# The last graph turn written out by hand, part of its routing moved into slices between the first expert units, unit rows in 38 buffers, landings looked up for 24 units

## The reference

```python
x = x + gnn(layernorm(x), adj, adj, ...)          # x: 128 graphs x 128 nodes x 128
# origin = where(adj <= 0, adj, 1); gnn: relu(((origin*adj) h + edge) * sigmoid(h g1 + b1)
#   + ((origin.T*adj) h + edge2) * sigmoid(h g2 + b2) + h * sigmoid(h g3))
xf = layernorm(x).reshape(-1, 128)                # 16384 tokens
top_w, top_i = top_k(xf @ Wg + bg, 2)             # the two largest of 8 logits
top_w = softmax(top_w)
for e in range(8):
    h = gelu(xf @ W1[e] + b1[e])                  # 128 -> 512, exact gelu
    out += w_dense[:, e:e+1] * (h @ W2[e] + b2[e])
return x + out
```

## Time and profile before

| | before |
|---|---|
| median of three runs | 720.95 us |
| the profiled execution, its time | 719.69 us |
| its span, first to last instruction | 717.8 us |
| busy: PE, DVE, ACT, POOL | 654.3, 608.5, 541.3, 504.2 us |
| share of the span on the chain that ended last: PE, ACT, POOL, issue, DMA, DVE | 32%, 23%, 13%, 12%, 10%, 8% |
| graph stage, to the first unit's layer 1 on PE | 0 to 214 us |
| first copy of a unit's output (`y_t`) | 225.88 us |
| DMA | 161.06 MB, 224 GB/s over the span |

### The profile page before, as it was taken

The page is one execution under the profiler, slowest core; times in us unless marked ns, Lnnn a source line. Parts: engine busy times, 40 slices in busy tenths (PEclk is TensorE's granted clock), DMA queues, the critical chain, the costliest instruction groups (busy, mean ns, idle before and its releaser), DMA issues.

```text
span 717.8 us, 17809 instructions
## 1 busy us (share of the span) xinstructions
PE 654.3 (91%) x4879; PEld 596.8 (83%) x4879; DVE 608.5 (85%) x2041; ACT 541.3 (75%) x1505; POOL 504.2 (70%) x471
## 2 busy tenths in 40 slices
PE   5979898988859999899997999988999999999991
PEld 4646566666539999899997999988999999999991
DVE  5899999999986888987885888885888888888881
ACT  4689999999977978788674767664777776767670
POOL 2553777676764577778887888877777777777774
PEclk9999999999977999999998999998999999999997
DMA  8999995558346897959999975789764444444211
GB/s 293 336 357 279 354 345 180 178 177 309 107 148 182 288 327 254 310 163 300 325 353 319 370 240 159 219 320 354 241 160 128 122 129 120 125 128 125 72 42 33
DMA packets 85497, 161.06 MB, mean 224 GB/s; under 512 B 32631, under 2 KB 36736, under 8 KB 85392
## 3 DMA queue, kind: packets, MB, share of 16 engines
q1 hardware_dynamic: 66032, 112.96, 50.2%
q0 software_dynamic: 18496, 46.70, 17.8%
q10 hardware_dynamic: 864, 0.21, 0.1%
HBM read 104.95 MB, written 57.23 MB: 226 GB/s over the span
## 4 chain that ended last, share of the span: by engine, by line
PE 32%; ACT 23%; POOL 13%; issue 12%; DMA 10%; DVE 8%; SPq 1%; POOLq 0%; DVEq 0%; ACTq 0%
POOL out_dram L688 8%; ACT hs L750 6%; POOL rows L691 5%; ACT row L759 5%; ACT t_loop L741 4%; PE bank L1623 4%; PE bank L1624 4%; PE bank L1625 4%; PE bank L1637 4%; PE bank L1638 4%; PE bank L1642 4%; ACT t_in L734 3%; DMA rows<-row,to_row 3%; PE bank L1609 2%; PE bank L1653 2%
## 5 line engine op out<-in xcount | busy, mean ns | idle before, releaser
L846 ACT ACTIVATE act_f<-bank,b_t 128x256 f32<-128x256 f32 x560 | 220.1, 476 | 22.8 <-PE bank L1625 14.7
L688 POOL DMA_INDIRECT out_dram<-row,to_row x140 | 165.7, 1184 | 57.7 <-issue 56.1
L646 POOL DMA_INDIRECT rows<-row,slot_low x128 | 136.8, 1069 | 62.6 <-issue 34.4
L1429 DVE TENSOR_TENSOR act_lo<-act_f,act_hi 128x1024 fp32r<-128x1024 f32 x140 | 171.9, 1228 | 5.9 <-ACT act_hi L852 0.2
L1422 DVE CAST act_hi<-act_f 128x1024 fp32r<-128x1024 f32 (+1 forms) x140 | 90.5, 647 | 70.1 <-ACT act_f L846 67.7
L836 ACT ACTIVATE in_hi<-bank 128x256 fp32r<-128x256 f32 x140 | 53.9, 385 | 113.4 <-PE bank L1609 113.1
L1623 PE MATMUL bank<-in_hi,w_t 128*128 128x256 f32 x376 | 115.6, 308 | 7.5 <-DMA w_t<-w_split 7.5
L691 POOL DMA_INDIRECT rows<-row,to_row x76 | 94.6, 1245 | 24.7 <-issue 20.9
L1624 PE MATMUL bank<-in_lo,w_t 128*128 128x256 f32 x376 | 107.4, 286 | 0.0
L1625 PE MATMUL bank<-in_hi,w_t 128*128 128x256 f32 x376 | 107.4, 286 | 0.0
L1637 PE MATMUL bank<-act_hi,w_t 128*128 128x256 f32 x376 | 100.9, 302 | 0.1
(11 more groups left out here) (278 smaller groups left out, 1762.2 us busy)
## 6 DMA issues: line engine op xcount, KB each, us to landing
row<-rows SPq DMA_DIRECT2D x108, 260.0 KB, 3.0
w_t<-w_split SPq DMA_DIRECT2D x52, 512.0 KB, 6.3
w_up<-w_split SPq DMA_DIRECT2D x28, 512.0 KB, 6.1
xs<-in_x_dram SPq DMA_DIRECT2D x16, 512.0 KB, 4.7
x_t<-in_x_turned_dram SPq DMA_DIRECT2D x16, 512.0 KB, 6.3
rows<-ends_rep SPq DMA_DIRECT2D x15, 260.0 KB, 7.7
xs<-rows SPq DMA_DIRECT2D x10, 260.0 KB
b_t<-in_biases_dram SPq DMA_DIRECT2D x140, 2.5 KB
```

What stands on the lines that cost most here:

```text
L646: pool.indirect_dma_start(out=rows, out_offset=bass.IndirectOffsetOnAxis(ap=slot_low[:, r, b:b + 1], axis=0), in_=row[:, r, b, :], in_offs ...
L688: pool.indirect_dma_start(out=out_rows, out_offset=at, in_=got[:, g, j, P:2 * P], in_offset=None, bounds_check=TOKENS - 1, oob_is_err=Fals ...
L846: last = act.activation(act_f[:, s, c, :], ps_h(t, half)[:, i, :], ACT.Gelu, bias=b_t[:, w, c:c + 1])
L1429: dve.tensor_tensor(act_lo[:, s], act_f[:, t.slot(2)], act_hi[:, s].bitcast(F32), ALU.subtract).then_inc(s_hlo, 1)
```

## The change

The last turn of the graph pipeline, which still held routing of chunk 12 and norms of chunk 14, is written out on PE, ACT and DVE without them. That work goes into the slices: the list on DVE is spread over k = 0 to 26 and has chunk 12's maxima (4), places (5), counts (6) and rows (7) in it, the norms of chunks 14 and 15 are done together (3), and chunk 13, 14 and 15 come later than before. NE becomes 34. Buffers for unit rows become 38 (LANES): 22 (FIRST) for the first 34 units in turn, and then all 38 in turn. For units 4 to 7 DVE casts the whole hidden layer, where ACT casts half of it for the other first units. On GpSimd the rows of chunk 12 come behind unit 4, the others are put elsewhere, and the landing of a unit is waited for and counted five units later in place of three. EARLY becomes 24.

```diff
-    EARLY = 3 * GR // 4
+    EARLY = 24
...
-    NE = 2 * GR
+    NE = 4 * FULL - (E - 2)
+    FIRST = 22
+    LANES = FIRST + GR
...
+    def lane(k):
+        return k % FIRST if k < NE else (FIRST + k - NE) % LANES
+    def uses(k):
+        return sum(lane(i) == lane(k) for i in range(k))
+    def halved(k):
+        return k < NE and not 4 <= k < 8
...
                     g = t.slot(GR)
-                    if not NE <= t.index < NE + GR:
-                        wait_slot(sp, s_out, 16 * BLK, t, 0)
+                    if uses(t.index):
+                        sp.wait_ge(s_out[lane(t.index)], 16 * BLK * uses(t.index))
...
-            now = entries(0, 0, NE, MOST, held=full_table)
+            now = entries(0, 0, UT, MOST, held=full_table) + entries(0, UT, NE - UT, MOST, held=full_table)
...
-            for k in range(CHUNKS - 3):
+            for k in range(CHUNKS - 4):
                 scatter_rows(chunk(k))
...
             def landed(t):
-                wait_slot(pool, s_out, 16 * BLK, t, 16 * BLK)
+                pool.wait_ge(s_out[lane(t.index)], 16 * BLK * (uses(t.index) + 1))
                 pool.sem_inc(s_landed, 1)
...
-                if 0 <= t.index - 3 < NU:
-                    landed(t.back(3))
+                if 0 <= t.index - 5 < NU:
+                    landed(t.back(5))
                 wait_turn(pool, s_done, 1, t, 1)
...
-            for k in range(6):
+            for k in range(5):
+                scatter(unit(k))
+            scatter_rows(chunk(CHUNKS - 4))
+            for k in range(5, 8):
                 scatter(unit(k))
             scatter_rows(chunk(CHUNKS - 3))
-            for k in range(6, 10):
+            for k in range(8, 11):
                 scatter(unit(k))
             scatter_rows(chunk(CHUNKS - 2))
-            for k in range(10, 14):
+            for k in range(11, 13):
                 scatter(unit(k))
             scatter_rows(chunk(CHUNKS - 1))
-            for k in range(14, UNITS):
+            for k in range(13, UNITS):
                 scatter(unit(k))
...
+            def last_turn(t):
+                two = t.back(1)
...
+                place_ranks(chunk(CHUNKS - 5))
+                place_rows(chunk(CHUNKS - 5))
+                for k in range(2):
...
+                    dve.tensor_tensor(t_sum[:, half, :], t_sum[:, half, :], t_loop[:, half, :], ALU.add).then_inc(s_tout, 1)
+                    if k == 0:
+                        wait_turn(dve, s_logit, 1, chunk(CHUNKS - 4), 1)
+                        dve.tensor_copy(full_table[:], ps_full_table).then_inc(s_full_tab, 1)
...
                 if k == 0:
                     last_sums(chunk(CHUNKS - 1))
                 elif k == 1:
+                    last_stats(chunk(CHUNKS - 2))
+                elif k == 2:
+                    last_stats(chunk(CHUNKS - 1))
+                elif k == 3:
+                    last_norms()
+                elif k == 4:
+                    last_maxima(chunk(CHUNKS - 4))
+                elif k == 5:
+                    last_two(chunk(CHUNKS - 4))
+                elif k == 6:
                     last_logits(chunk(CHUNKS - 3))
-                    last_stats(chunk(CHUNKS - 1))
...
+                    last_counts(chunk(CHUNKS - 4))
+                elif k == 7:
+                    place_ranks(chunk(CHUNKS - 4))
+                    place_rows(chunk(CHUNKS - 4))
```

More of the change, by code:

```diff
@@ L400, in program @@
         s_done = sem("unit_summed")
-        s_out = [sem(f"unit_rows_scattered{i}") for i in range(GR)]
+        s_out = [sem(f"unit_rows_scattered{i}") for i in range(LANES)]
         s_landed = sem("first_pass_units_landed")
@@ L600, in _ @@
                         rows_in(unit(k + AHEAD), early[k + AHEAD - NU] if 0 <= k + AHEAD - NU < AHEAD else now[i])
-            for i in range(GR):
-                sp.wait_ge(s_out[i], 16 * BLK * ((UNITS + GR - 1 - i) // GR))
+            for k in range(UNITS - LANES, UNITS):
+                sp.wait_ge(s_out[lane(k)], 16 * BLK * (uses(k) + 1))
         @block.gpsimd
@@ L1166, in full_units @@
                 dve.scalar_tensor_tensor(out=full_code[:, 0:1], in0=start_, scalar=16.0, in1=new_, op0=ALU.mult, op1=ALU.add).then_inc(s_full_code, 1)
-            for k in range(CHUNKS + 2):
+            for k in range(CHUNKS + 1):
                 until = turn(chunk(k), until)
@@ L1420, in hidden_hi @@
                 wait_turn(dve, s_act, 2, t, 2)
-                done = FC // 2 if t.index < NE else 0
+                done = FC // 2 if halved(t.index) else 0
                 dve.tensor_copy(act_hi[:, t.slot(LATE + 1), done:], act_f[:, t.slot(2), done:]).then_inc(s_hhi, 1)
@@ L1426, in hidden_lo @@
                 wait_turn(dve, s_hhi, 1, t, 1)
-                if t.index < NE:
-                    wait_turn(dve, s_half, 1, t, 1)
+                if halved(t.index):
+                    dve.wait_ge(s_half, sum(halved(i) for i in range(t.index + 1)))
                 dve.tensor_tensor(act_lo[:, s], act_f[:, t.slot(2)], act_hi[:, s].bitcast(F32), ALU.subtract).then_inc(s_hlo, 1)
             def sum_up(t):
-                g, second = t.slot(GR), int(t.index >= NU)
+                g, second = lane(t.index), int(t.index >= NU)
                 held = rows_of_unit(t)
@@ L1552, in _ @@
             pe.matmul(ps_mean, mean_m[:], gate_w[:], start=True, stop=True).then_inc(s_mean, 1)
-            for k in range(CHUNKS + 2):
+            for k in range(CHUNKS + 1):
                 turn(chunk(k))
+            final, two = chunk(CHUNKS - 1), chunk(CHUNKS - 3)
+            inner(final, 1)
+            outer(final, 1)
+            ranks(chunk(CHUNKS - 5))
+            for k in range(2):
+                logits(chunk(CHUNKS - 4), k)
+            transposed(two, lambda b: row[:, two.index % RING, b, 0:P], s_h2, s_h2t_ps, (s_h2t, 2, two), -1)
             def turned_rows(t, k):
@@ L1631, in layer2 @@
                 wait_turn(pe, s_hhi, 1, t, 1)
-                if t.index < NE:
-                    wait_turn(pe, s_half, 1, t, 1)
+                if halved(t.index):
+                    pe.wait_ge(s_half, sum(halved(i) for i in range(t.index + 1)))
                 wait_turn(pe, s_y, 1, t, 0)
```

193 lines of the change are left out of this document (109 added, 84 removed).

## The result

The changed kernel takes 730.57 us (median of 4 runs, 729.03 to 732.11); the kernel before, on the same chip, 720.36 us (4 runs, 717.55 to 721.79). The ratio is 1.0146, 95% interval 1.0124 to 1.0168: slower by some 10 us. 735 was predicted, with 717 to 743 as range. The profiled execution took 730.92 us, its span is 729.2 us, against 719.69 and 717.8 before: 11.2 us on the execution's own time, where the sum gave 15.8.

The account below looks back on a forecast made before the run. GpSimd's scatter list, held to 3.20 us a unit by DVE's subtraction, was taken to set the second pass. Unit 66's landing is passed on at 497.7 where it was 481.9: +15.8 on 719.69 gives 735.5, or 735; range 717 to 743.

Parts of the forecast that it names:

- GpSimd's list sets the second pass: GpSimd's scatters up to unit 66's landing set the second pass's start; chunk 12's eight scatters add 11.2 us.
- The lock: On GpSimd, every second scatter waits for DVE's subtraction to end, so a unit takes 3.20 us in place of 2.54.
- The sum that met 477.90 with 478.5: Check on the kernel before: GpSimd's list from 252.18, priced by scatter, ends at 478.5; the row says 477.90.
- The buffers: With 38 buffers the 6.5 us stall ahead of unit 44 goes, but PE's gain is lost in a longer wait.
- Landings five back: GpSimd passes on unit 66's landing only after issuing unit 70, two more units of its list, at 497.7.
- PE's arrival: PE, if nothing holds it, reaches unit 75's first layer at 482.9 - 6.5 + 2 = 478.4, then idles some 20 us.
- the sum's own rule: A microsecond saved or lost on PE moves the end by 1 - 2.54 / 3.20 = 0.2 us only.
- The slices: Between the first units, a fourth chunk's routing joins three: 2 us taken, bounds 0 to 3.7.
- Look-ups for 24 units: SP's count of landed units looked up for 24 second-pass units: worth nothing, the wait is for unit 78.
- rivals, 1 to 3: 1: GpSimd gets loose, 712, chance 0.12; 2: halfway at 3.0 us, 727, 0.18; 3: cast holds scatters, 732, 0.08.
- Rival 4: The second pass no longer waits for the big expert's landings: 708 us, chance 0.04.
- Rival 5: Slices cost all, and GpSimd's pace is 3.26 us throughout: 744 us, chance 0.04.

Follow-up runs that it names:

- e6: e1 with chunk 12's eight scatters issued a second time on GpSimd, between units 4 and 5: 731.43 us, ratio 1.0153.
- e4: The changed kernel with DVE's subtraction done as two instructions of half the length: 722.30 us, ratio 1.0032.
- e1: The kernel before with 38 buffers, NE = 34, landings five back, 24 look-ups; its last turn, slices and GpSimd order kept: 721.13 us.
- e7: e1 with DVE's subtraction in two halves: 719.69 us, ratio 0.9989.
- e9: e7 with landings counted three units back in place of five: 714.58 us, ratio 0.9929.
- e5: The kernel before once more, nothing changed but a comment: 719.43 us, ratio 0.9994.
- e2: The changed kernel with landings waited for three units back in place of five: 732.27 us, ratio 1.0157.
- e10: e4 with landings counted three units back in place of five: 720.54 us, ratio 1.0013.
- e8: The kernel before, 16 buffers, with DVE's subtraction in two halves: 709.57 us, ratio 0.9855.

## Why the prediction was right, and where it was not

**GpSimd's list sets the second pass: right, and shown.** e6 moves the list alone and gets the changed kernel's time; e4 frees the list and takes most of the loss back. Unit 13 was forecast at 318.6 and started at 319.59. At 478.4, the moment for which the sum put GpSimd at unit 62.9, unit 63 was about to start (479.00). The lock was forecast at 3.20 us a unit and measured 3.14 in the mean, 3.28 where PE has no gaps. Of its details one was misread: the held scatter ends 0.85 us behind the subtraction in the earlier trace rows, not 0.97 (332.10 + 1.67 against 331.69 + 1.23). The sum that met 477.90 with 478.5 is weaker support than it looks, since the 3.20 in it was read from the same stretches.

**The buffers: right.** The gap ahead of unit 44 went, and PE's gain was lost in a longer wait (e1). Six gaps of 0.35 to 1.85 us, 5.4 in all, which the sum did not have, came in its place.

**Landings five back: the step that failed.** The term was "two more units of its list", 5.1 us, and the whole passage that lets the count of unit 66 come only when unit 70 is issued. In the changed kernel it came 0.03 us behind the landing, at 491.27; the wait was forecast to end at 497.7. Taking the landing in place of unit 70, the sum's own terms give 478.4 + 3.6 x 2.54 + 3.99 = 491.5. That this meets the 491.27 is partly luck: the scatter went out 1.3 us later than so reckoned and landed 1.6 us sooner (2.42 in place of 3.99). The trace of before showed the step already: the scatter of unit 66 landed at 481.89 and the weights behind SP's wait were issued at 482.88, when GpSimd's timeline had come to unit 68's first scatter, and unit 68's own turn has the count of unit 65 with three back:

```profile
482.31 0.97 POOL L691 DMA_INDIRECT rows<-row,to_row  x1 [0.30 <-issue]
```

I took the place of the count in the list for the time at which it runs; the sequencer that runs it is several units ahead of the scatters when these queue up. e7 and e9 show where the term is real: 5.1 us, in a kernel whose GpSimd keeps up.

**PE's arrival: misread, mis-sized, and of little effect.** PE was to be at unit 75's first layer at 478.4 and came at 487.6, so it idled 8.1 us and not some 20. Of these 9.2 us 0.7 are a misreading: the 4.1 us of the earlier trace rows are unit 45's wait at 381.79, while at unit 75 PE waited 3.43 and was there at 483.64, not 482.9. For the other 8.4 the traces have 8.9: 2.5 from the start and the slices (unit 27's copy came 4.5 us later than before, at 330.24, where 2 was taken), 47 units by 0.032 = 1.5 from the pace, 5.2 from the six gaps (over the new pace), and 0.3 less ahead of units 72 and 73; the half microsecond too many stays open. By the sum's own rule, a microsecond on PE moves the end by 0.2 us only: 1.8 of them.

**The slices: too small.** The first output came 3.8 us earlier than before, at 222.06, outside the 2 us allowed; but it moves by itself (224.18 in e5 against 225.88, and 223.17 to 223.93 in e2, e4 and e10, which have the change's last turn), so that some 2 us of it are the change's. The 27 units behind it took 108.2 us where they took 99.9. The bound of 3.7 was taken from one more chunk on top of three; the 8.3 us, 7.4 of them slices and 0.9 pace, are twice that. e10 less e9 puts the net price, with the earlier start in it, at 6.0 us. In the changed kernel it does not show, GpSimd being later still.

**The pace: not seen at all.** Allocating 38 buffers made every unit 0.032 us longer. Behind the restart there are 65 units: 2.1 us, which with the 9.4 us of SP's later restart make 11.5; the spans differ by 11.4.

**Look-ups for 24 units: nothing, as forecast:** one wait for the count, ahead of unit 78's rows, as before. No run takes this part out by itself.

Two errors thus stood against each other: 6.2 us too many for the count (497.7 against 491.5), 2.1 us too few for the pace. Without the first, 729.3 would have been forecast. Of the rivals, 1 to 3 needed a GpSimd that gets looser, by phase or by the cast. It got loose only beside PE's gaps, for nine units, so that 3.14 us was the mean; the scatter through the cast was not held; none of the three came, and e4 shows what loosening is worth when it is made to happen. Rival 4 fell with SP's wait, which ended with unit 66's landing. Rival 5's slices were as dear as it said or dearer, but GpSimd hid them.

## What to carry to other kernels

When an engine's list sets the time, look for what holds each of its instructions: here one DVE instruction, cut into two at a cost of 0.07 us, gave 10 us back (e8, 709.57 us, where the kernel before took 719.93 and the changed one 730.57). Extra buffers ahead of such an engine only moved the wait (e1), and work put into its list cost nearly its full length (in e6 9.1 us at unit 13, 8.4 at the second pass), even if it could stand where the engine has nothing to do. The place of a wait in a list tells when it runs only if the engine stands there: first see whether the engine lags.

## What had not been expected of the hardware

- A scatter that began some 0.4 us into DVE's subtraction of two 128x1024 SBUF operands took 1.68 us, one clear of it 0.97; with the subtraction in two halves, together 0.07 us longer, 1.43 at most (e4, 320 to 460 us). A cast of 0.69 us, of one SBUF operand, did not lengthen the scatter that ran through it (0.98 us).
- The allocation of unused bytes ahead of PE's operands changed the rate of its matmuls at an unchanged granted clock: 1034, 1028 or 1024 in 120 us.
- GpSimd's count of a landing ran 0.03 us behind the landing while the scatters were at unit 67, three units short of the count's place in the list; where GpSimd waited for sums, SP's load behind the count went out 14 us behind the unit's first scatter (e7).
